# Mixture-of-experts kernel: 25 whole blocks and 11 couples of half blocks in place of 39 whole blocks, and one group of tokens chosen and ranked a step earlier

## The reference, cut to what matters

```
logits = einsum('bsd,de->bse', input_emb, Wr) + br        # E = 8 experts
route_w = softmax(logits);  topk_idx = top_k(route_w, 2)   # two experts of each token
routed = route_w * mask / sum(route_w * mask)
h = relu(einsum('bsd,edh->ebsh', input_emb, W1) + b1)      # 128 -> 512
expert_out = einsum('ebsh,ehd->ebsd', h, W2) + b2          # 512 -> 128
return einsum('bse,ebsd->bsd', routed, expert_out)
```

## Time and profile before

| | |
|---|---|
| time, median of 3 runs | 353.44 us (353.34 to 354.66) |
| the profiled execution's own time | 355.26 us |
| its span, first to last instruction | 353.5 us |
| PE, DVE, ACT, POOL busy | 83%, 81%, 63%, 71% |
| mean granted PE clock | 0.922 of full |
| expert blocks | about 203 us to 330 us of the span |

### The profile page before, as it was taken

How to read it: one execution, slowest core, us unless ns; L and a number is a source line. 1 busy time by engine, 2 the same in 40 slices (tenths; PEclk the granted TensorE clock), 3 DMA queues, 4 the chain that set the end, 5 groups by cost and what they waited for, 6 DMA issues and landing times.

```text
span 353.5 us, 7837 instructions
## 1 busy us (share of the span) xinstructions
PE 294.8 (83%) x2237; PEld 209.9 (59%) x2237; DVE 285.2 (81%) x623; ACT 222.9 (63%) x644; POOL 249.3 (71%) x251
## 2 busy tenths in 40 slices
PE   5899999989979999799867699999999999997000
PEld 5677845545545555555424477778888888886000
DVE  5888899999886999999899549997777777772196
ACT  2688711488878745245434886768888888882092
POOL 4639995454979998898777477777777777777300
PEclk9899999999999999899969589999999999997555
DMA  8990000000000000001111266525655454411397
GB/s 227 351 289 19 2 0 0 0 4 0 1 0 0 2 23 26 23 23 53 56 45 52 48 98 109 100 71 96 103 100 107 107 100 108 105 58 52 106 401 236
DMA packets 50026, 29.16 MB, mean 82 GB/s; under 512 B 34993, under 2 KB 44639, under 8 KB 49986
## 3 DMA queue, kind: packets, MB, share of 16 engines
q1 hardware_dynamic: 45142, 19.02, 22.4%
q0 software_dynamic: 4544, 9.38, 9.5%
q10 hardware_dynamic: 300, 0.27, 0.2%
HBM read 10.87 MB, written 12.67 MB: 67 GB/s over the span
## 4 chain that ended last, share of the span: by engine, by line
PE 41%; DVE 29%; issue 10%; ACT 9%; POOL 8%; DMA 2%; POOLq 0%; ACTq 0%; DVEq 0%; SPq 0%
PE ps L1260 9%; POOL y_rows L554 7%; PE ps L1259 5%; DVE nd L914 4%; DVE work L903 4%; PE ps L1233 3%; PE ps L1421 3%; PE ps L1423 2%; PE ps L1422 2%; DVE rows L930 2%; PE ps L1440 2%; PE ps L1441 2%; PE ps L1445 2%; DVE x L1194 2%; DVE wraw L1145 2%
## 5 line engine op out<-in xcount | busy, mean ns | idle before, releaser
L554 POOL DMA_INDIRECT y_rows<-kvt,yid x78 | 74.7, 958 | 23.8 <-issue 21.3
L520 POOL DMA_INDIRECT x_rows<-rows,pos_i x64 | 62.4, 975 | 21.7 <-issue 17.8
L722 ACT ACTIVATE ps<-ps,b1s 128x256 f32<-128x256 f32 x156 | 60.4, 451 | 16.3 <-PE ps L1423 14.1
L1145 DVE TENSOR_TENSOR wraw<-ps,wraw 128x1024 f16<-128x1024 f32 x39 | 47.7, 1224 | 21.1 <-ACT wraw L728 20.8
L1421 PE MATMUL ps<-wraw,w1h 128*128 128x256 f16 x156 | 43.3, 278 | 0.8 <-issue 0.6
L1423 PE MATMUL ps<-wraw,w1l 128*128 128x256 f16 x156 | 43.1, 276 | 0.0
L1422 PE MATMUL ps<-wraw,w1h 128*128 128x256 f16 x156 | 43.1, 276 | 0.0
L914 DVE TENSOR_REDUCE nd<-work 128x144 f32<-128x1152 f32 x32 | 41.8, 1346 | 0.4
L1440 PE MATMUL ps<-w,wraw 128*128 x312 | 40.4, 221 | 0.0
L1441 PE MATMUL ps<-w,wraw 128*128 x312 | 40.4, 222 | 0.0
L903 DVE TENSOR_TENSOR work<-ps,qk 128x1024 f32<-128x1024 f32 x32 | 37.9, 1214 | 2.2 <-PE ps L1260 2.2
(11 more groups left out here) (243 smaller groups left out, 741.0 us busy)
## 6 DMA issues: line engine op xcount, KB each, us to landing
qk<-y_rows SPq DMA_DIRECT2D x8, 512.0 KB, 6.5
wraw<-in_L_ffn_W_dram SPq DMA_DIRECT2D x1, 2048.0 KB, 11.1
out_dram<-x SPq DMA_DIRECT2D x8, 256.0 KB, 4.2
x<-in_L_attn_x_dram SPq DMA_DIRECT2D x3, 512.0 KB, 7.0
y_rows<-kvt,yid POOLq DMA_INDIRECT x78, 2.4
x_rows<-empty SPq DMA_DIRECT2D x9, 130.0 KB, 3.4
x_rows<-rows,pos_i POOLq DMA_INDIRECT x64, 2.3
wraw<-x_rows SPq DMA_TRANSPOSE x39
```

Source lines behind the costliest of these rows:

```text
L520: nc.gpsimd.indirect_dma_start(out=x_rows, out_offset=bass.IndirectOffsetOnAxis(ap=pos_i[:, c, t:t + 1], axis=0), in_=rows[:, t, :], in_of ...
L554: nc.gpsimd.indirect_dma_start(out=y_rows, in_=ysb[:, n % YG, g], in_offset=None, out_offset=bass.IndirectOffsetOnAxis(ap=yid[:, n, g:g + ...
L722: ins = nc.scalar.activation(o, o, ACT.Relu, bias=b1s[:, bass.ds(e * HC + c, 1)])
L1145: nc.vector.tensor_tensor(hl[:, n % HB], inner(n), hh[:, n % HB], ALU.subtract).then_inc(lo_done, 1)
```

## The change

The blocks are now of two kinds. NF = 25 whole blocks (13 of part 0 and 12 more) are followed by NH = 11 couples: a couple is a block of 256 slots whose two halves of 128 rows may belong to two experts. With units of 128 rows fewer slots stay empty, and NBLK is 36. The table of the second part has one entry for a whole block and two for a couple, and making it takes more DVE instructions (`second_full`, `second_used`, `second_halves`, `second_choice`), so it is ready one block later (SPREAD 7 for 6). In a couple each instruction that names an expert stands twice, once per half. Apart from that, group FIRST is chosen and ranked inside step 15, and the first table's broadcast goes to the bank `ps[:, 0]` that held prefix sums. POOL's `power_2` now stands ahead of the scatters of its step in steps 13 to 15 too.

```diff
-    NBLK = TOP * NT // GPB + E - 1
-    N2 = NBLK - N1
+    N2 = (PAIRS - N1 * SLOTS - E * (SLOTS - 1) + SLOTS - 1) // SLOTS
+    NF = N1 + N2
+    HALVES = (PAIRS - NF * SLOTS - E) // P + E
+    NH = (HALVES + 1) // 2
+    NBLK = NF + NH
+    NE2 = N2 + 2 * NH
+    ENTRIES = N1 + NE2
-    SPREAD = 6
+    SPREAD = 7
-        w1h = sb("w1h", [P, E, HID], F16)
-        w1l = sb("w1l", [P, E, HID], F16)
+        w1 = sb("w1", [P, E, 2, HID], F16)
+        def parts(n):
+            return 1 if n < NF else 2
...
+                for h in range(k):
+                    slots = slice(h * P, (h + 1) * P) if k == 2 else slice(0, SLOTS)
...
+                    sp.dma_start_transpose(xgT[:, b, :, slots], rows_of_block[:, 0:D].bitcast(F16)).then_inc(x_turned[b], 16)
...
-                if 2 <= s < 13:
+                if s >= 2:
                     power_2(s - 2)
...
-                if s >= 13:
-                    power_2(s - 2)
...
+                if s == U - 1:
+                    statistics(s - 1)
                 if s - 3 in ended_by:
                     copy_logits(ended_by[s - 3])
...
                 for c in range(HC):
                     at = c % 2 * SLOTS
-                    o = ps[:, 2 * (n % HB) + c // 2, at:at + SLOTS]
-                    ins = nc.scalar.activation(o, o, ACT.Relu, bias=b1s[:, bass.ds(e * HC + c, 1)])
+                    for h in range(k):
+                        o = ps[:, 2 * (n % HB) + c // 2, at + h * P:at + (SLOTS if k == 1 else (h + 1) * P)]
+                        ins = nc.scalar.activation(o, o, ACT.Relu, bias=b1s[:, bass.ds(e[h] * HC + c, 1)])
...
+            def second_used():
+                link(nc.vector.tensor_tensor_scan(second[:, 0], ones[:, 0:E], full, 0.0, ALU.mult, ALU.add))
+                link(nc.vector.tensor_tensor(second[:, 1], second[:, 0], full, ALU.subtract))
+                link(nc.vector.tensor_scalar(used[:, 0], second[:, 0], float(N2), None, ALU.min))
+                link(nc.vector.tensor_scalar(used[:, 1], second[:, 1], float(N2), None, ALU.min))
+                link(nc.vector.tensor_tensor(used[:, 0], used[:, 0], used[:, 1], ALU.subtract))
+                link(nc.vector.tensor_tensor(used[:, 1], used[:, 0], used[:, 2], ALU.add))
...
+                if s == U - 1:
+                    table_copies(0)
+                    choose_first(FIRST)
+                    choose_second(FIRST)
                 reduce(s, 0)
...
+                if s == U - 1:
+                    positions(FIRST)
                 reduce(s, 1)
-                if s == U - 1:
-                    table_copies(0)
                 quotient(s)
...
-            choose_first(FIRST)
-            choose_second(FIRST)
-            positions(FIRST)
...
                 elif s == U - 1:
+                    logits(s - 3)
+                    ranks(FIRST)
                     pe.wait_ge(table_done, 2)
-                    logits(s - 3)
...
+                for h in range(parts(n)):
+                    for w in range(2):
+                        pe.lower_ap(second_layer(n, h, c, w))
+                    if c == HC - 1:
+                        pe.lower_ap(second_bias(n, h))
...
                 for c in range(HC):
+                    for h in range(k):
+                        slots = slice(h * P, (h + 1) * P) if k == 2 else slice(0, SLOTS)
+                        xh, xl = xgT[:, n % XG, 0, slots], xgT[:, n % XG, 1, slots]
+                        at = c % 2 * SLOTS
+                        o = ps[:, 2 * (n % HB) + c // 2, at + slots.start:at + slots.stop]
+                        wh, wl = first_layer(n, h, c, 0), first_layer(n, h, c, 1)
+                        nc.tensor.matmul(o, wh, xh, start=True, stop=False)
+                        nc.tensor.matmul(o, wh, xl, start=False, stop=False)
+                        ins = nc.tensor.matmul(o, wl, xh, start=False, stop=True)
...
             pe.wait_ge(x2T_out, U - 3)
-            ranks(FIRST)
-            pe.wait_ge(rank_out, FIRST + 1)
             turn_x2(U - 3)
```

More of the change, by code:

```diff
@@ L359, in slots_of, with entry, arrived, table_of @@
             return slice(first, first + group_tiles(g) + 1)
+        def entry(n):
+            return n if n < NF else NF + 2 * (n - NF)
+        def parts(n):
+            return 1 if n < NF else 2
+        def arrived(n):
+            return 16 * sum(parts(m) for m in range(n % XG, n + 1, XG))
         def routed(g, at, n):
-            if g > FIRST or g == FIRST and at >= RANK:
+            if g > FIRST or g == FIRST and at >= COUNT:
                 return ps[:, 6, at:at + n]
             return ps[:, 7, T + at:T + at + n]
+        def table_of(i, n):
+            flat = routed(FIRST, TABLE, 5 * n) if i else ps[:, 0, 0:5 * n]
+            return flat.rearrange("p (k n) -> p k n", k=5)
         @block.sync
@@ L1011, in table_expert @@
             def table_expert(i):
+                last = second[:, 0] if i else ends
                 if i == 0:
@@ new lines, in second_halves @@
+            def second_halves():
+                half = t8[:, 2, 0]
+                link(nc.vector.tensor_scalar(cnt_i[:, :], second[:, 2], float(P - 1), None, ALU.add))
+                link(nc.vector.tensor_scalar(cnt_i[:, :], cnt_i[:, :], P.bit_length() - 1, None, ALU.logical_shift_right))
+                link(nc.vector.scalar_tensor_tensor(out=half, in0=used[:, 1], scalar=-2.0, in1=cnt_i[:, :],
+                                                    op0=ALU.mult, op1=ALU.add))
+                link(nc.vector.tensor_tensor_scan(other[:, 0], ones[:, 0:E], half, float(N2), ALU.mult, ALU.add))
+                link(nc.vector.tensor_tensor(half, other[:, 0], half, ALU.subtract))
+                link(nc.vector.scalar_tensor_tensor(out=other[:, 1], in0=used[:, 1], scalar=-2.0, in1=half,
+                                                    op0=ALU.mult, op1=ALU.add))
+                link(nc.vector.tensor_tensor(second[:, 1], second[:, 1], used[:, 2], ALU.subtract))
@@ L1429, in down @@
             def down(n):
+                if n >= NBLK - 2:
+                    expert_of_second(n)
                 if n >= 1:
                     pe.wait_ge(y_out, n)
+                k = parts(n)
                 both = ps[:, 7, 0:GPB * D].rearrange("p (g d) -> p g d", g=GPB)
-                nc.tensor.matmul(both, ones_b[:, :], second_bias(n), start=True, stop=False)
                 outs = [ps[:, 7, g * D:(g + 1) * D] for g in range(GPB)]
+                for h in range(k):
+                    nc.tensor.matmul(both if k == 1 else outs[h], ones_b[:, :], second_bias(n, h), start=(h == 0), stop=False)
                 pe.wait_ge(hi_done, n + 1)
```

221 lines of the change are left out of this document (123 added, 98 removed).

## The result

The changed kernel takes **377.51 us** (median of 4 runs, 375.58 to 377.71), the kernel before 354.05 us (4 runs). The ratio is **1.063, with a 95% interval of 1.0594 to 1.0665**. The forecast was 373.1 us in a range of 362 to 380, with 0.95 for slower. Side and range hold, and both causes are seen in the traces; one term, that of the couples, was too small by 4 us (16.2 for 20.3).

The account below looks back on a forecast made before the run. PE was taken to fill each 2.84 us block, its sequencer close behind, with DVE setting the pace ahead of the blocks. To 353.4 were added 8.9 + 2.2 + 0.9 - 8.5 + 16.2 + 0.8 - 0.8 = +19.7: 373.1 us, range 362 to 380.

Parts of the forecast that it names:

- The last step, +8.9: Step 15 on DVE: choosing ahead of the reductions waits for logits, so y_s and block 0 start late; +8.9 us.
- POOL's order at nothing: POOL in steps 13 to 15: part 0's rows out about five us later, costing nothing while block 0 is late.
- Longer table +2.2: DVE between blocks 1 and 6: 11 more instructions for the second table, not hidden; +2.2 us, between 1 and 2.7.
- whole blocks +0.9: PE in whole blocks: longer register instructions cost some 0.05 us a block over 20 blocks; +0.9 us, between 0 and 2.
- Three blocks, -8.5: Block loop: three blocks fewer at 2.84 us each; -8.5 us.
- Couples on PE, +16.2: PE in the couples: sequencer's address instructions lengthen a slot from 2.84 to 4.4 us; +16.2 us, bounds 9 and 21.
- Couples at array time: Rival, couples: they cost only array time, ACT then bounds at 3.2 us a slot; 359.1 us, chance 0.09.
- Choosing hidden: Rival, last step: the choosing is hidden after all, since PE's ranking goes too; 364.2 us, chance 0.07.
- The falling clock: Rival, couples on PE: clock falls to half for a third to all of the slots; 377 to 384 us, chance 0.10.
- POOL's queue: Rival, POOL's scatters: their queue sets the end, and six fewer give -7.6, so 345.8 us; chance 0.03.
- Both losses small: Rival, last step and couples: the two losses at their lower bounds; 352 to 357 us, chance 0.03.
- The tail: The end: more address instructions in the last two blocks, +0.8 us; POOL no longer behind, -0.8 us.

Follow-up runs that it names:

- e3b: Kernel before with 39 whole blocks, only choosing and ranking of the late group moved into the last step, second sort of chip: 1.0205 times the kernel before.
- e9: Changed kernel with choosing, ranking and POOL's order as before, and both couple halves on the first half's expert on PE (output changes), second sort: 0.9817 times kernel before.
- a0: The changed kernel itself, unaltered, on a chip of the second sort: 1.0082 times the kernel before.
- e5: Changed kernel with separate address calls for couples' first-layer weights, 16 more PE register instructions a couple, first sort: 393.78 us, 1.1077 times the kernel before.
- e6: Changed kernel with one ACT relu of 256 columns a chunk of a couple in place of two (output changes), first sort: 376.71 us, 1.0607 times kernel before.
- e1: Changed kernel with choosing and ranking put back behind the last step, POOL's new order kept, second sort: 0.9983 times the kernel before.
- e2b: Changed kernel with choosing and ranking behind the last step and POOL's powers and scatters ordered as before, repeat run, second sort: 1.003 times the kernel before.
- e4b: Changed kernel with both couple halves on the first half's expert on PE (output changes), repeat run, second sort: 0.9802 times the kernel before.
- e7: Changed kernel with both couple halves on the first half's expert on PE and one ACT relu a chunk (output changes), second sort: 0.982 times kernel before.

## Why the prediction was right, step by step

*The last step, +8.9: right, +9.0.* `y_s` was put at 203.0 and stands at 202.84, block 0 at 212.1 and stands at 212.19. The idle time of DVE ahead of the choosing is the step that carried it. e3b gives the same size where nothing else is changed, but on the second sort and by way of POOL's scatters, so that the two numbers agree is in part luck. The sum gave the chain behind `y_s` no slack. That holds on the chip that was profiled; on the second sort only 2 to 4 us of the loss are left in the changed kernel.

*POOL's order at nothing: right here.* Part 0's last scatter starts at 198.70 in place of 194.01, 4.7 us late for the 5 that were said. Its cover, the late block 0, was there: SP's first transposing DMA of a block stands at 202.05 in place of 197.4, still 10 us ahead of block 0's first matmul (212.19), which has no idle time before it. On the second sort the same order gives time back, as far as the traces tell.

*Longer table +2.2 and whole blocks +0.9: together 1.7* (from block 0's copy to block 22's). The sum was an over-estimate by 1.4. From block 8's copy to block 22's the 14 blocks take 0.5 us more, 0.04 each where I had 0.05. Up to block 8, where the table is made, it is 1.2 in all. So the table was put too high: it is near the lower bound of 1. The register instruction ahead of the low weight, REGISTER_ALU in the order of the program, stands in the trace of before as the first of these rows and has become the second, of the kind that the order calls ISA:

```profile
L1423 PEldq ALU_OP  x156: 32/32/42, 203.2 to 317.2; - x156
```
```profile
L1519 PEldq FUSED_REGOPS  x188: 46/46/51, 212.2 to 339.3; - x188
```

So it is 14 ns longer. Behind the load of the registers the changed kernel's trace has one of 38 ns (L1475, x34), before's a MOVE of 29 (L1393, x39).

*Three blocks, -8.5:* as counted.

*Couples on PE, +16.2: the mechanism right, the size too small; it is +20.3.* This is the mis-sized term. The step that failed is "I take 1.2" for the rest of a slot, with 0.30 for the load of the registers and 0.13 for an address of the longer kind. A slot is 4.75, not 4.4. The second layer with the load and the waits is 1.47, which is most of the miss, and the first layer 3.3 in place of 3.15. The two first slots were to be 3.9 because they hold fewer addresses, and are 4.62 and 4.21. Nine slots at 0.35 and these two, 1.0 together, are the 4.1 us. That the sequencer and not the array or ACT sets the slot is shown from both sides: twelve instructions fewer took 1.0 us off a slot (e9 against a0; at least, as the chip's own pace then binds), sixteen more put 1.5 on it (e5 at full clock), and half of ACT's relus did nothing (e6). What was added in e5 is worth 0.08 to 0.10 us for each instruction.

The 0.125 us of the earlier trace rows comes back in the couples: between the last matmul of a half and the first of the next, with a register instruction between them, the trace has 0.12 (309.73 to 309.85), where matmuls within a half are 0.06 apart.

*The rivals.* Couples at array time (359.1): out. Choosing hidden (364.2): out on this chip. The falling clock (377 to 384): the time, 377.5, lies at the start of its range, but the window above shows 1.00 throughout, so it was not the cause, and that the time touches this range is chance; the clock fell one dose further, in e5. POOL's queue: out, POOL waits for ACT in the couples. Both losses small: out.

*The tail:* +1.1 for +0.8, and -1.1 for -0.8. *The base:* I added to 353.4 while the profiled execution of before stood 1.8 higher, which is the other part of the miss: 22.5 measured on profiled executions for 19.7, and 1.8 of base, make 373.1 into the 377.7 of that execution. The table's over-estimate of 1.4 hid a part of what the couples lacked, which is luck.

## What to carry to other kernels

Before splitting matmuls into smaller ones with weights chosen at run time, count the register instructions on PE's queue: here they came at 0.08 to 0.14 us each (0.08 to 0.10 in e5, 0.12 to 0.14 between most starts in the changed kernel's trace) where matmuls of 128 columns start 0.056 apart, and 25 of them in a slot, where 13 had been, cost more than three whole blocks saved. Moving work "early" in a queue moves whatever it waits for in front of all that stands behind it: look at when its input comes before asking how long it takes; here the wait was 3.95 us and the work 3.6. And a cost that is fully on the path on one chip can be covered on another (9.0 us and 2 to 4 here), so the changed kernel itself belongs beside every variant of it. And a wait that the profile puts down to "remote" is first looked up in the code: the semaphore it waits for names the engine to ask.

## What the runs showed of the hardware

*Two sorts of chips.* The same program takes 354 us or 417 us. The engines' own times are alike in the changed kernel's trace and in a0's: POOL's issue of a scatter of y 0.958 and 0.957 us (median of 72), ACT's copy 0.38 on both, PE's second layer from the bias to the end of its last matmul 1.63 and 1.62. What differs is PE's signal. On the first sort `down_done` rises 0.01 us after the end of PE's row (median over the blocks, in before, after, e5 and e6); on the second sort it rises 1.45 to 1.56 us after it (the same median in a0, e1, e2b, e3b, e4b, e7 and e9). A whole block of a0, PE's row and the copy that waits for it:

```profile
300.50 0.61 PE L1545 MATMUL ps<-w,wraw 128*128 x8
```
```profile
302.61 0.38 ACT L773 ACTIVATE kvt<-ps 128x256 f32<-128x256 f32 x1 [0.84 <-PE ps L1545]
```

This is enough for the 3.6 us a block. The next second layer starts when this copy is done (303.05 behind 302.61 + 0.38); it takes 1.6, its signal 1.5 and the copy 0.4, together 3.5. On the first sort the same round is 2.0 and hides behind PE's 2.84. In a0's couples the signal is at most 0.3 behind, and the slot is 4.7 on both sorts. Whether the signal is late or the profile has PE's row too early, and whether the chip, its memory or a neighbour makes the difference, isn't settled by these runs.

*Landings.* The expectation of a0 has scatters of y landing 6.6 to 7.3 us after their issue on the second sort, and 2.7 on the first. Those figures are from the view by tile, which counts SP's eight loads of the results in with the scatters. The pages keep them apart; first the changed kernel on the first sort, then a0 (tiles, engine, operation, KB each, median us to landing):

```profile
qk<-y_rows SPq DMA_DIRECT2D x8, 512.0 KB, 6.7
...
y_rows<-kvt,yid POOLq DMA_INDIRECT x72, 2.4
```
```profile
qk<-y_rows SPq DMA_DIRECT2D x8, 512.0 KB, 6.5
...
y_rows<-kvt,yid POOLq DMA_INDIRECT x72
```

The 6.6 to 7.3 are the loads' times, and on the first sort the loads take 6.5 (before) and 6.7. For the scatters the first sort has 2.4, and the traces of the second sort have no landing of any. So no run shows that POOL's scatters land later there.

*A clock that fell.* In e5 PE was busy for 7.1 to 8.3 us of 10 on matmuls of 128 columns, and the granted clock of such stretches was 1.00, 0.83, 0.83 and 0.73 of full. These are means of two levels, 1.00 and 0.50, the only ones in the trace: between 294 and 296 it was 0.50, between 298 and 306 it was 1.00. In the changed kernel's couples, with PE busy for 38.2 of 46 us (296 to 342), it was 1.00 throughout.
